# Token experts of an audio tower: the second layer's weights become the fixed matrix, gates are spread over partitions through DRAM, sums are turned back once per sequence

## The reference

```python
def _L1_ffn_ref(x, gate_w, gate_b, w1, b1, w2, b2):      # E = 8 experts, K = 2, H = 128, 2H = 256 inner units
    logits = jnp.einsum('bsh,he->bse', x, gate_w) + gate_b
    topk_vals, topk_idx = jax.lax.top_k(logits, K)
    topk_weights = jax.nn.softmax(topk_vals, axis=-1)
    weights = ...                                        # zero for the six experts that a token did not choose
    h = jax.nn.relu(jnp.einsum('bsh,ehf->bsef', x, w1) + b1)
    expert_out = jnp.einsum('bsef,efh->bseh', h, w2) + b2
    return jnp.einsum('bseh,bse->bsh', expert_out, weights)
h = h + _L1_ffn_ref(_layernorm(h, axis=-1), ...)         # the last line of the tower
```

## Time and profile before

| | |
|---|---|
| median of 3 runs | 2229.58 us (2226.82 to 2231.67) |
| the profiled execution | 2227.92 us, its span 2225.8 us |
| mean granted TensorE clock | 0.963 of full |
| TensorE busy with products / weight loads | 1999.1 us (90%) / 1774.5 us (80%) |
| VectorE, ScalarE, GpSimd busy | 1572.6, 1069.0, 645.4 us |
| first hidden piece of the tail, last store of the tail | 1512.07 us, 2221.72 us |

### The profile page before, as it was taken

The page is one execution under the profiler, slowest core; times in us unless marked ns, Lnnn a source line. Parts: engine busy times, 40 slices in busy tenths (PEclk is TensorE's granted clock), DMA queues, the critical chain, the costliest instruction groups (busy, mean ns, idle before and its releaser), DMA issues. The chain is left out here.

```text
span 2225.8 us, 54751 instructions
## 1 busy us (share of the span) xinstructions
PE 1999.1 (90%) x20890; PEld 1774.5 (80%) x20890; DVE 1572.6 (71%) x4080; ACT 1069.0 (48%) x2699; POOL 645.4 (29%) x856
## 2 busy tenths in 40 slices
PE   8599999989656889986999999968999999999998
PEld 6497777779545888874777777758999999999998
DVE  5745655654584765665999999977777777777774
ACT  4433333332344565653677777743444344444443
POOL 0202222220015555521444444442122212221220
PEclk9799999999867999998999999988999999999999
DMA  8100011100211111100000000000000000000000
GB/s 187 46 1 12 12 14 13 13 6 1 75 56 40 42 40 39 40 19 1 3 3 3 3 3 4 3 2 1 15 7 7 7 14 7 7 7 14 7 8 15
DMA packets 80550, 44.51 MB, mean 20 GB/s; under 512 B 45867, under 2 KB 74091, under 8 KB 80011
## 3 DMA queue, kind: packets, MB, share of 16 engines
q1 hardware_dynamic: 73416, 29.26, 5.8%
q0 software_dynamic: 5888, 12.07, 2.1%
q10 hardware_dynamic: 1024, 0.26, 0.1%
HBM read 27.20 MB, written 14.38 MB: 19 GB/s over the span
## 5 line engine op out<-in xcount | busy, mean ns | idle before, releaser
L2139 ACT ACTIVATE w<-banks,b 128x384 f32<-128x384 f32 (+1 forms) x512 | 259.4, 572 | 392.9 <-PE banks L2214 392.9
L2196 PE MATMUL banks<-w,w 128*128 128x128 f32 (+1 forms) x3072 | 364.1, 276 | 0.0
L2196 PEld LDWEIGHTS banks<-w,w 128*128 128x128 f32 (+1 forms) x3072 | 350.5, 189 | 9.1 <-issue 8.7
L1693 POOL TENSOR_TENSOR t<-eb 128x256 f32<-128x256 f32 (+1 forms) x288 | 199.5, 726 | 248.8 <-ACT eb L1668 210.8
L1722 PE MATMUL banks<-qT,w 64*64 64x128 f32 (+1 forms) x4608 | 265.8, 268 | 4.2 <-ACT eb L1668 2.4
L1730 PE MATMUL banks<-eb,w 64*64 64x128 f32 (+1 forms) x4608 | 268.9, 270 | 0.5 <-DVE eb L1622 0.3
L1722 PEld LDWEIGHTS banks<-qT,w 64*64 64x64 f32 x4608 | 245.7, 133 | 21.0 <-issue 13.8
L1730 PEld LDWEIGHTS banks<-eb,w 64*64 64x64 f32 x4608 | 244.1, 133 | 1.3 <-DVE eb L1622 1.1
L2036 DVE SCALAR_TENSOR_TENSOR h<-banks,t_wt,h 128x128 f32 (+3 forms) x672 | 183.7, 343 | 82.6 <-PE banks L2196 79.1
L1247 POOL DMA_INDIRECT xg<-xs,rowu x184 | 180.7, 982 | 128.6 <-DMA xg<-xs,rowu 84.7
L1622 DVE TENSOR_TENSOR eb<-eb,rd 128x1536 f32<-128x1536 f32 x96 | 192.0, 2000 | 9.3 <-ACT rd L1679 8.1
(11 more groups left out here) (305 smaller groups left out, 4240.1 us busy)
## 6 DMA issues: line engine op xcount, KB each, us to landing
out<-h SPq DMA_DIRECT2D x16, 320.0 KB
xs<-r_xl SPq DMA_DIRECT2D x16, 192.0 KB, 2.7
xg<-xs,rowu POOLq DMA_INDIRECT x184, 2.6
h<-in_xT SPq DMA_DIRECT2D x3, 750.0 KB, 14.5
h<-in_xT SPq DMA_DIRECT2D x3, 749.0 KB, 17.6
xs<-r_xl SPq DMA_DIRECT2D x16, 128.0 KB
blocks<-NT SPq DMA_DIRECT2D x24, 48.0 KB, 1.9
D<-blocks SPq DMA_DIRECT2D x24, 48.0 KB, 2.1
```

What stands on the lines that cost most here:

```text
L1693: nc.gpsimd.tensor_tensor(t1[:, n % 2, 0:m, 2 * s:2 * s + 2].rearrange("p t v -> p v t"), e[:, v:v + 2, 0:m], e[:, v + 2:v + 4, 0:m], ALU. ...
L2139: nc.scalar.activation(gb[u % 2][:, f, s * GW:s * GW + NFREE[s]], k.ps[:, order.bank(n), 0:NFREE[s]], ACT.Relu, bias=k.b1_1[:, 2 * e + f:2 ...
L2196: last = nc.tensor.matmul(k.psf[0:n, o:o + P], gb[u % 2][:, f, c * P:c * P + n], k.w2_1[:, 2 * e + f, :], start=(f == 0), stop=(f == 1))
```

## The change

Four things change together.

1. **The output's operands change places.** The second layer's weights are loaded and `gb` moves, 384 or 362 columns at a time: 4 products (8 instructions) for a unit, and the result has the channels on the partitions.
2. **The gates become a matrix.** A gate now belongs to a column, so all 128 partitions need it. `wT`, the turned gates (48 x 128), is written to DRAM once per sequence, and for each unit SyncE's queue reads the expert's rows back to all partitions into `wtb[u % 2]` (384 KB). For this `weigh` moves from e = 1 to e = 0, `wT` to the middle of the hidden pieces of e = 0, and `logits` to the middle of those of e = 7; the exponent moves to the end of e = 7.
3. **Multiply and add are two steps.** VectorE multiplies PSUM by `wtb` into `parts` (shown as `video`, whose room it takes) and adds that to `sums`: four instructions for a unit, two for a sequence's first.
4. **The sums turn back.** When a sequence's eight units are done, TensorE turns its `sums` (two "back" pieces, six transposes) at e = 2 of the next sequence, and VectorE adds them to `h` in three instructions; the last sequence's come at the end. The stores move behind that. `hx` goes; the tokens are added in `h` itself.

```diff
-            out += [("hidden", x, u) for x in range(4)]
+            out += [("hidden", x, u) for x in range(2)]
+            if e == 0:
+                out.append(("wT", 0, u))
+            if e == 7 and front:
+                out.append(("logits", 0, u))
+            out += [("hidden", x, u) for x in range(2, 4)]
...
             if e == 2:
-                out.append(("wT", 0, u))
+                out += [("back", g, u) for g in range(2)]
...
+                for b in range(B):
...
+                    sp.wait_ge(free, order.emptied(i, order.find("wT", 0, par, last_pair), False, last_pair))
+                    sp.dma_start(gates, wT[:]).then_inc(gates_out, 16)
+                    sp.wait_ge(gates_out, 16 * (b + 2))
+                    for e in range(E1):
+                        n = b * E1 + e
+                        if n >= 2:
+                            sp.wait_ge(added, n + 1)
+                        row = gates.rearrange("(c e) t -> e c t", e=E1)[e]
+                        sp.dma_start(wtb[:, n % 2], row.partition_broadcast(P)).then_inc(gates_in[n % 2], 16)
+                        if e == 5 and b:
+                            store(b - 1)
...
                 def gated(i, u, last_pair):
                     par, e = divmod(u, E1)
                     dve.wait_ge(o_ps, i * U + (u + 3))
+                    dve.wait_ge(gates_in[u % 2], i * (8 * U) + 16 * (u // 2 + 1))
                     if e:
-                        dve.wait_ge(added, i * U + (u + 2))
-                    for c in range(NC):
...
-                        last = nc.vector.scalar_tensor_tensor(out=hh, in0=k.psf[0:n, o:o + P],
-                                                              scalar=wt[0:n, par, c * E1 + e:c * E1 + e + 1],
-                                                              in1=hh if e else hx[0:n, c, :], op0=ALU.mult, op1=ALU.add)
+                        dve.wait_ge(folded, i * (2 * MORE) + (par * MORE + e))
+                    acc = sums[:, par]
+                    gate = wtb[:, u % 2].rearrange("p c t -> p (c t)")
+                    for s in range(2):
+                        at = slice(s * GW, s * GW + NFREE[s])
+                        last = nc.vector.tensor_tensor(parts[:, at] if e else acc[:, at],
+                                                       k.ps[:, 4 + u % 2 * 2 + s, 0:NFREE[s]], gate[:, at], ALU.mult)
                     last.then_inc(added, 1)
+                    if e:
+                        dve.wait_ge(added, i * U + (u + 3))
+                        for s in range(2):
+                            at = slice(s * GW, s * GW + NFREE[s])
+                            last = nc.vector.tensor_tensor(acc[:, at], acc[:, at], parts[:, at], ALU.add)
+                        last.then_inc(folded, 1)
...
-                        if e == 1:
+                        if e == 0:
                             weigh(i, par)
-                            if front:
-                                linear_sum(i, par + 1)
+                        if e == 1 and front:
+                            linear_sum(i, par + 1)
                         if e == 2 and front:
                             norm_sum(i, par + 1)
+                        if e == 2:
+                            back(i, par, last_pair, first)
...
+                    for s in range(2):
+                        w = NFREE[s]
+                        for f in range(2):
+                            last = nc.tensor.matmul(k.ps[:, 4 + u % 2 * 2 + s, 0:w], k.w2_1[:, 2 * e + f, :],
+                                                    gb[u % 2][:, f, s * GW:s * GW + w], start=(f == 0), stop=(f == 1))
+                    last.then_inc(o_ps, 1)
```

More of the change, by code:

```diff
@@ L335, in over_pairs, with first_then_pairs @@
     body(PAIRS - 1, True)
+def first_then_pairs(eng, body):
+    body(0, False, True)
+    with eng.Fori(1, PAIRS - 1) as i:
+        body(i, False, False)
+    body(PAIRS - 1, True, False)
 class NormTranspose:
@@ L1769 @@
                 ("logits", 0, 0)]
-    BY_VECTOR = ("lin", "logits", "bias")
+    BY_VECTOR = ("lin", "logits", "bias", "back")
     def __init__(self):
@@ L1894, in _, with store @@
                 clear_stale(sp, k)
-                for b in range(B):
-                    sp.wait_ge(added, E1 * (b + 1) + 2)
+                def store(b):
+                    i, par = divmod(b + 1, 2)
+                    if i < PAIRS:
+                        last_pair = i == PAIRS - 1
+                        sp.wait_ge(freed, order.emptied(i, order.find("back", 1, par, last_pair), True, last_pair))
+                    else:
+                        sp.wait_ge(freed, order.emptied(PAIRS - 1, len(order.ending) - 1, True, True) + 2)
                     sp.dma_start(k.out[b, 0:T - LAST, :].rearrange("(c p) d -> p c d", p=P),
@@ new lines, in back @@
+                def back(i, par, last_pair, first):
+                    n = order.find("back", 0, par, last_pair)
+                    if first and par == 0:
+                        for g in range(2):
+                            dve.wait_ge(full, order.filled(i, n + g))
+                            nc.vector.memset(blank[:, g:g + 1], 0.0).then_inc(freed, 1)
+                    elif par:
+                        returned(seq(i, 0), i, n, last_pair,
+                                 order.emptied(i, order.find("bias", 1, 0, last_pair), True, last_pair))
+                    else:
+                        returned(seq(i, -1), i, n, last_pair, order.emptied(i, -1, True) - 1)
@@ L2042, in body @@
+                def body(i, last_pair, first):
                     for u in range(U):
@@ L2071, in _ @@
                 rank(0, 0)
-                over_pairs(dve, body)
-                dve.wait_ge(added, B * E1 + 2)
+                first_then_pairs(dve, body)
+                end = len(order.ending)
+                returned(B - 1, PAIRS - 1, end, True,
+                         order.emptied(PAIRS - 1, order.find("bias", 1, 1, True), True, True))
+                dve.wait_ge(freed, order.emptied(PAIRS - 1, end - 1, True, True) + 2)
             @block.gpsimd
@@ L2222, in body @@
                                              start=True, stop=True).then_inc(full, 1)
+                        elif kind == "back":
+                            if first and par == 0:
+                                nc.tensor.transpose(k.ps[:, bank, 0:P], k.ident[:, :], k.ident[:, :]).then_inc(full, 1)
+                            else:
+                                pe.wait_ge(folded, i * (2 * MORE) + (par * MORE + 1))
+                                turn_back(1 - par, x, bank)
                         else:
@@ L2237, in _ @@
                 pe.wait_ge(w_split, 2)
-                over_pairs(pe, body)
+                first_then_pairs(pe, body)
+                end = len(order.ending)
+                pe.wait_ge(free, order.emptied(PAIRS - 1, end - 1, False, True))
+                pe.wait_ge(folded, B * MORE + 1)
+                for x in range(2):
+                    turn_back(1, x, order.bank(end + x))
 def audio_tower(nc, a, out):
@@ L2344, in audio_tower @@
         k.blocks = nc.dram_tensor("blocks", (2, 4, 12, 32, 32), F32, kind="Internal").ap()
+        k.gates = nc.dram_tensor("token_gates", (2, NC * E1, P), F32, kind="Internal").ap()
         k.lists = nc.dram_tensor("lists", (2, 2, E0 * (B // 2) * CAP), F32, kind="Internal").ap()
```

80 lines of the change are left out of this document (51 added, 29 removed).

## The result

The changed kernel takes **2375.94 us** (median of 4 runs, 2374.83 to 2382.24) against 2230.62 (2226.82 to 2234.38) for the kernel before on the same chip: ratio 1.0662, interval 1.0645 to 1.0679, 145 us slower. The profiled execution took 2374.83 us with a span of 2372.6 us and a mean granted clock of 0.942, so the spans of the two profiled executions differ by 146.8 us. The forecast was 2350, between 2298 and 2398.

The account below looks back on a forecast made before the run. The tail was taken as one chain of TensorE, where waits for VectorE are paid in full. 65 + 16 + 8 + 10 + 3 + 2.5 - 9 = +95 us, plus 26 for the clock, on 2227.9: 2350 us, range 2298 to 2398.

Parts of the forecast that it names:

- `turn_x`: TensorE's existing 0.57 us wait for VectorE before this turn grows, as the gating ahead is 0.53 longer: +8 us.
- The output pass: TensorE's output of a unit takes 2.52 us instead of 2.59: -9 us, between -10 and +40.
- Gating 2.08 a unit: VectorE's multiply 1.0, add 1.0 and a wait between: 2.08 us, +0.53 for each unit but a sequence's first.
- The wait at the turn: TensorE waits for VectorE's `weigh` at the turn of `wt`, 4.4 or 3.7 us a sequence: +65 us, the largest term.
- The returned sums: Hidden piece 2 of e = 3 waits 1.1 us for VectorE to add the first back piece, fifteen times: +16 us.
- The transfers: The gates' reads of 384 KB a unit stay hidden, with 3 us of cover at the first unit: nothing added.
- rival (b): The gates come late through SyncE's queue; a read of 8 us would give 2385 to 2400; chance 0.12.
- The clock: TensorE falls to half clock after each of 16 new waits, judged by a row of 4.81 us idle: +26 us.
- (a): Rival: TensorE's waits come as forecast but the clock stays: 2323 us; chance 0.32.
- (c): Rival: VectorE keeps up, `weigh` is ready, and only TensorE's own work changes: 2234 us; chance 0.03.
- (d): Rival: wide output products run one column a cycle, 0.17 us each, an output 1.36: 2201 us; chance 0.05.
- (e): Rival: the waits are half as long, as VectorE's instructions overlap more: 2270 to 2300 us; chance 0.13.

Follow-up runs that it names:

- experiment 2: The changed kernel with VectorE's loop over the pairs written out, so without its jump back: 2353.83 us, ratio 1.0555.
- experiment 4: The changed kernel with the two back pieces and VectorE's addition of the returned sums moved from e = 2 to e = 3: 2351.65 us, ratio 1.0550.
- version 5: The changed kernel with `weigh` directly behind `rank`, the returned sums at e = 3 and VectorE's loop written out: 2275.56 us, ratio 1.0209.
- version 11: version 5 with the gating of the unit before placed in VectorE's waits for GpSimd's power and `norm_tokens` a unit earlier: 2239.02 us, ratio 1.0049.
- experiment 3: The changed kernel with TensorE transposing the identity as filler while it waits for the gates' turn: 2360.55 us, ratio 1.0597.
- experiment 6: The changed kernel with VectorE's addition of the parts to `sums` cut to two columns, result incomplete: 2323.47 us, ratio 1.0419.
- experiment 8: The kernel before with one more 384-wide fp32 addition on VectorE per unit and the gating wait also at e = 0: 2237.06 us, ratio 1.0034.

## Why the prediction was right, and where its sizes were off

**The bound.** That the tail is one chain of TensorE, in which a wait for VectorE is paid in full, held: the waits, the clock and the terms of TensorE's own work sum to the difference. With what was measured: 85.5 (turn of `wt`) + 39 (clock) + 13 (returned sums) + 9 (`turn_x`, 17.8 - 8.6) + 13 (transposes and changes of kind, taken as forecast) + 2.6 (end) - 20 (outputs) = 142, against 146.8 of the spans. The rest is about what the waits cost beyond their shown length: a wait is counted from the recorded end of the product before it, which holds 0.17 us of pipeline, and there are 48 waits against 16, so 32 x 0.17 = 5 us (an estimate).

**The output pass, forecast -9, measured -20.** Its pace was forecast right. Within an output the next product starts 0.32 us behind one of 384 columns and 0.30 behind one of 362, so eight take 2.51, where the working had 2.50. Two neighbours of one output, then its last product and the first pass of the next hidden piece:

```profile
1854.70 0.49 PE L2276 MATMUL banks<-w,w 128*128 128x384 f32 x1
1855.02 0.49 PE L2276 MATMUL banks<-w,w 128*128 128x384 f32 x1
...
1856.25 0.47 PE L2276 MATMUL banks<-w,w 128*128 128x362 f32 x1
```

The hidden piece is recorded as started at 1856.28, only 0.03 behind the eighth product, and then takes 0.46 to its second pass instead of 0.17. The 0.29 more is the eighth product's own time, shown upon the piece behind it: 2.23 + 0.29 = 2.52. In the same way the slow first pass in the earlier trace rows, 0.26 instead of 0.17, is the time of the last of the 24 old products. The working took that 0.09 off the old output and counted 2.59, where 2.59 + 0.09 = 2.68 stands against the new 2.52: -0.16 a unit instead of -0.07. So the term mis-sized was the old output, not the new one, and by luck in the direction that made up for part of the waits. The 0.37 that held the upper bound is a product with a change of kind at its side; the two between the edges of the earlier trace rows take 0.32 as well.

**Gating 2.08 a unit** was right to the row: 1833.06 to 1835.16 is 2.10. Left out was that some additions of the second pass are slow: 16 of 224 last 1.33 to 1.35 us instead of 0.53 to 0.56, so the mean in the group of L2081 is 605 ns and the median 557.

**The wait at the turn, forecast 65, measured 85.5.** For a pair's second sequence 4.4 was forecast and 5.08 measured in six of eight, 37.8 us in all against 35; for its first 3.7 was forecast and 7.0 to 7.1 measured in five of eight, 47.7 in all against 30. So nearly all that was missed lies at the first sequences. The working put `weigh` directly behind the two gatings. Left out were the jump back of VectorE's loop, 2.35 us (experiment 2), and about 1.0 us of lateness with which the first of the two gatings starts (1833.06, 0.84 before TensorE is at the turn; the forecast had it 1.84 before). The two first sequences inside the tail that have no jump before them, with waits of 4.4 and 4.6, agree with the second of these. In the old order `weigh` stood at e = 1, and a pause at the loop's end met nobody waiting: the trace of before has it, 1.6 us ahead of `weigh`'s first step, with ScalarE named as releaser.

```profile
1695.45 0.17 DVE L2008 TENSOR_SCALAR t_pm<-t_mx 128x6 f32<-128x6 f32 x1 [1.60 <-ACT t_mx L2143]
```

Why the second sequences wait 0.7 longer than forecast was not worked out. The sign "a pair 13 to 16 us longer" missed for the same reasons: it was 20.4.

**The returned sums, forecast 16, measured 13.1** in 14 places of up to 1.0 us; moving them gave 24 (experiment 4), so the trace's wait understates what the place costs. **`turn_x`, forecast +8, measured +9.**

**The transfers, forecast hidden.** A read took 6.5 us from issue to landing, not the 4.5 assumed (the write before it 1.4, not 2.3), and still VectorE waited for them only 7.9 us in all. That the lateness of VectorE itself gave the cover is argued, not shown, but it fits: the waits grow as VectorE gets earlier, to 18.4 us in version 5 and 40 in version 11. The price of rival (b) was set too high: by the forecast's own cover of 3 us a read of 8 us, 3.5 over the assumed, would come 0.5 late, 8 us in sixteen and not 32 to 48.

**The clock, forecast 26, measured 39.** It fell behind the waits of 7.0 and 5.1 us, as taken from the row of 4.81. Its price was taken from 3.3 us at half pace, 1.65 lost; here the half pace lasts 5.3 and 4.4 us, 2.65 + 2.2 = 4.85 a pair, 39 in eight. Eight times one pair is a little much, since the first two pairs and the last differ; the starts of all products give 37 more than before (an estimate). Only 15 to 25 of it come back with the fillers (experiment 3). The Trainium skill (TensorE: Matmul & The Clock Gate, Part 1) has the half clock as the default that activity releases. The trace agrees in that the half clock stood behind both waits, of 5 and 7 us, that the windows show. Behind waits of 3.09 us in version 5 it stood in one place and not in another, and behind one of 2.5 us in experiment 6 it stood again, so the length of a wait alone does not tell.

**The rivals.** (a) fell by the windows at 0.50. (b), late gates, fell for this kernel, though the end result of 2376 lies near its 2385 and by time alone could not be told from it; the list of waits tells. (c) fell: VectorE keeps up only where `rank`, gating and `weigh` aren't between TensorE and its next need (experiment 8 shows that order, +8). (d) fell at 0.30 to 0.32 a product against its 0.17. (e) fell: the waits were longer, not shorter.

## What to carry to other kernels

An engine with spare time in the sum can still be the bound at one handover: a us of VectorE's work cost 0.14 us in the order with slack and 0.4 to 0.6 where its result was needed two pieces after it could start. When a change moves a consumer forward, work out the producer's whole queue up to that point, with loop ends and what other changes add to it; and mend all such places before judging the idea, since one mended place lets the next one show, and since the price of the half clock need not fall with a single edit (2, 5 and 7 us came back for one each, 29 for the three together). When work is read from starts, add the slow first pass behind a piece to that piece. Rows with a small wait that comes back every round (0.57 us here, fifteen times) are worth an edit of one line.

## What the runs showed of the hardware that was not expected

- At the jump back of VectorE's loop over pairs nothing runs for 2.35 us, with no releaser shown; with the loop written out the longest wait of TensorE falls by 2.0 us and the kernel by 22 us. The idle time there differs with what VectorE still has to do when its sequencer jumps: 1.2 us in experiment 8, 2.9 to 3.3 in experiment 6. From the branch's own record (which no view lists) to the first instruction of the new round it is 3.0 to 3.4 us in all of them, and 3.0 in the kernel before (1692.46 to 1695.45).
- Waits of TensorE of 3.09 us left the clock at 1.00 in one place and were followed by a mean of 0.61 in another; one of 2.5 us was followed by 3.4 us at 0.50; waits of 5.0 and 7.0 us by 4.4 and 5.3 us at 0.50.
- A wide fp32 product takes 0.32 us for 384 columns and 0.30 for 362, 0.84 ns a column; one of 128 columns takes 2.68 / 24 = 0.112, 0.87 ns a column. The last of a row is recorded 0.03 us before the next kind's first product, which then holds its time: 0.46 to the next start behind wide products, 0.26 behind narrow ones, 0.17 otherwise.
- An fp32 addition on VectorE with both inputs in SBUF can be slow beside an instruction of GpSimd. In the changed kernel 31 of the 224 additions of L2081 overlap such an instruction by over 0.05 us; 16 of them last 1.33 to 1.35 us and 14 last 0.65 to 0.66, while none of the other 193 lasts over 0.56. The multiplication of L2074, which reads PSUM, stays at 0.56 or less though 30 of its instructions overlap too. Here two additions take 1.80 us together instead of 1.00, beside GpSimd's 1.00. What this costs the kernel was not tried; in version 5, where 30 additions last 1.33 to 1.35, it is some 24 us of VectorE's time (30 x 0.79, an estimate).

```profile
1873.52 1.00 POOL L2171 TENSOR_TENSOR t_xlo<-t_xT,t_xh 128x384 fp32r<-128x384 f32 x1 [2.54 <-ACT t_xh L2197]
1873.58 1.80 DVE L2081 TENSOR_TENSOR t_sums<-t_sums,video 128x384 f32<-128x384 f32 x2
```
